# A graph network on one core: attention finishes each target tile inside its loop

## What is computed

```python
Q = (hn @ Wq).reshape(n, H, HD)          # K and V alike; hn = batch_norm(h)
score = jnp.clip(jnp.einsum('ehd,ehd->eh', K[src], Q[dst]) / np.sqrt(HD), -5.0, 5.0)
a = jnp.exp(score - smax[dst])
a = a / asum[dst]
wV = segment_sum(V[src] * a[:, :, None], dst, num_segments=n).reshape(n, DIM)
h2 = h_in1 + wV @ Wo + bo
h3 = _batch_norm(h2, bn2_g, bn2_b)       # statistics over all nodes
h3 = jax.nn.relu(h3 @ W1 + b1) @ W2 + b2
return h2 + h3                           # then a layer norm, and the last layer
```

## Time and profile before

| | |
|---|---|
| median of three runs (lowest to highest) | 1334.77 us (1333.79 to 1335.28) |
| profiled execution, its own time | 1335.18 us |
| its span, first to last instruction | 1333.2 us |
| busy: TensorE, VectorE, ScalarE, GpSimd | 990.6, 867.2, 523.6, 413.0 us |
| first and last gather of the loop start at | 655.7 and 1175.5 us |

### The profile page before, as it was taken

How to read it: one execution, slowest core, us unless ns; L and a number is a source line. 1 busy time by engine, 2 the same in 40 slices (tenths; PEclk the granted TensorE clock), 3 DMA queues, 4 the chain that set the end, 5 groups by cost and what they waited for, 6 DMA issues and landing times. The chain is left out here.

```text
span 1333.2 us, 18242 instructions
## 1 busy us (share of the span) xinstructions
PE 990.6 (74%) x6074; PEld 622.3 (47%) x6074; DVE 867.2 (65%) x2126; ACT 523.6 (39%) x1007; POOL 413.0 (31%) x516
## 2 busy tenths in 40 slices
PE   1289989999999998894655565656656565557997
PEld 1168845645556454454433343434434333345554
DVE  4879946734434467466377877777877777764343
ACT  1289913111111111112456555556655556424210
POOL 4000000000000000001277777777777777720000
PEclk9999999999999999896865766666666766568999
DMA  6000061000000000000543333333333333319000
GB/s 156 26 1 1 1 211 34 1 9 0 9 1 0 17 16 23 12 1 24 154 123 104 106 106 104 106 105 106 107 105 106 107 105 105 107 44 226 12 24 26
DMA packets 49496, 87.78 MB, mean 66 GB/s; under 512 B 12384, under 2 KB 35315, under 8 KB 49161
## 3 DMA queue, kind: packets, MB, share of 16 engines
q0 software_dynamic: 20608, 55.20, 14.4%
q1 hardware_dynamic: 26312, 29.89, 8.3%
q10 hardware_dynamic: 2492, 1.61, 0.5%
HBM read 70.68 MB, written 15.98 MB: 65 GB/s over the span
## 5 line engine op out<-in xcount | busy, mean ns | idle before, releaser
L1413 POOL DMA_INDIRECT counts_all<-kv_d,counts_all x416 | 394.4, 948 | 154.7 <-issue 145.9
L867 PE MATMUL bank<-counts_all,parts 125*128 (+2 forms) x1750 | 344.4, 355 | 19.5 <-DVE parts L1047 9.7
L867 PEld LDWEIGHTS bank<-counts_all,parts 125*128 125x128 f16 x1750 | 159.8, 98 | 190.9 <-DVE parts L1047 11.0
L1553 PE MATMUL bank<-counts_all 125*128 125x128 f16 x1230 | 133.9, 288 | 83.3 <-ACT counts_all L1619 82.9
L1299 POOL IOTA iota_n<- 128x256 f16 x1 | 0.3, 349 | 562.1 <-POOLq L854 562.1
L1553 PEld LDWEIGHTS bank<-counts_all 125*128 125x128 f16 x1230 | 110.1, 133 | 126.6 <-ACT counts_all L1619 126.3
L1542 PE MATMUL bank<-rel_rows,ident_h 104*128 104x512 f16 x104 | 56.9, 547 | 124.6 <-ACT away L1609 123.9
L1483 DVE TENSOR_TENSOR counts_all<-counts_all,bank 128x512 f32<-128x512 f32 x104 | 71.5, 687 | 117.6 <-DMA counts_all<-kv_d,counts_all 117.6
L1568 PE MATMUL bank<-counts_all,parts 128*128 128x272 f16 x615 | 135.2, 378 | 14.3 <-DVE counts_all L1461 12.1
L670 PE MATMUL bank<-parts 128*125 128x125 f16 x625 | 102.7, 324 | 12.0 <-DVE parts L589 12.0
L1609 ACT ACTIVATE away<-bank,lane_bias 125x512 f16<-125x512 f32 x173 | 110.8, 680 | 1.0 <-PE bank L1542 0.7
(11 more groups left out here) (268 smaller groups left out, 1264.2 us busy)
## 6 DMA issues: line engine op xcount, KB each, us to landing
counts_d<-counts_all SPq DMA_DIRECT2D x1, 6835.9 KB
counts_all<-counts_d SPq DMA_DIRECT2D x1, 6835.9 KB
counts_all<-kv_d,counts_all POOLq DMA_INDIRECT x416
kv_d<-counts_all SPq DMA_DIRECT2D x6, 448.0 KB
q_d<-counts_all SPq DMA_DIRECT2D x1, 1562.5 KB
x<-in_x SPq DMA_DIRECT2D x6, 250.0 KB
out<-parts SPq DMA_DIRECT2D x6, 250.0 KB
inv_deg<-in_x SPq DMA_DIRECT2D x1, 1400.0 KB
```

Of the source, the lines that this page charges most:

```text
L867: last = T.matmul(agg_ps[p][:, 0:w], pin[:, s, part, :], counts[:, s, bass.ds(b * BLK, w)], start=(s + part == 0), stop=(s + part == NT))
L1413: G.indirect_dma_start(out=out_rows, out_offset=None, in_=table_d, in_offset=bass.IndirectOffsetOnAxis(ap=index, axis=0)).then_inc(signal, 16)
L1553: last = T.matmul(pick_ps[n % DEEP][:, k * C:(k + 1) * C], ohT[n % DEEP][:, tile - GTILES[n][0], k, :], Q[:, tile, part, :], start=(tile = ...
```

## The change

Division, turning, projection and statistics move from the next stage into the loop. For a tile whose last group is L, ScalarE copies the high half in iteration L + 3 and VectorE adds the low half; VectorE divides in L + 4; TensorE turns the tile in L + 6 and ScalarE copies it; TensorE projects it in L + 7 and ScalarE copies that; VectorE takes its statistics in L + 8. Tiles 0 to 22 get through in the loop, 23 and 24 (`LATE`) right behind it. `turn_ps` and `project_ps` are in the bank that the spread writes, so in those two iterations the spread goes behind ScalarE's copy. `Q` and the projected tiles `h2T` share the end of the counts' room, so the counts come back in four pieces, three behind an `ff_done`. The general path gets the same steps, written out for 25 tiles.

```diff
+        ARENA_END = NT * N - NT * 2 * C - (NT * N) % 16
+        turned_area = counts_all[:, ARENA_END:ARENA_END + NT * 2 * C]
+        Q = turned_area[0:TILE, :].rearrange("p (t h c) -> p t h c", h=2, c=C)
+        h2T = turned_area.bitcast(fp32).rearrange("p (t c) -> p t c", c=C)[:, :, 0:TILE]
...
+            TURN_AT = {LAST_OF[t] + 6: t for t in range(NT) if LAST_OF[t] + 7 < NG}
+            PROJECT_AT = {LAST_OF[t] + 7: t for t in range(NT) if LAST_OF[t] + 7 < NG}
+            STATS_AT = {LAST_OF[t] + 8: t for t in range(NT) if LAST_OF[t] + 8 < NG}
...
+            LATE = [t for t in range(NT) if LAST_OF[t] + 7 >= NG]
...
+            turn_ps, project_ps = ps[0][:, 0:TILE], ps[0][:, LANES:LANES + TILE]
...
+                    sp.dma_start(w1[:, :], W1).then_inc(ff_in, 16)
+                    sp.dma_start(w2[:, :, :], W2.rearrange("(j f) c -> f j c", j=2)).then_inc(ff_in, 16)
                     sp.wait_ge(cols_in, 16 * 7)
...
+                    def divide(tile):
+                        rden_st.run(V.tensor_scalar(rden, acc[:, tile, C:VW], 1e-20, att_scale[0:TILE, V_SCALE:V_SCALE + 1],
+                                                    ALU.max, ALU.mult))
+                        rden_st.run(V.reciprocal(rden, rden))
+                        wv = acc[:, tile, 0:C].rearrange("p (h c) -> p h c", h=HEADS)
+                        V.tensor_tensor(wv, wv, rden.unsqueeze(2).to_broadcast([TILE, HEADS, HD]), ALU.mult).then_inc(wv_ready, 1)
+
+                    def statistics(tile):
+                        dve.wait_ge(h2_copied, tile + 1)
+                        V.bn_stats(bst2[:, tile, :], h2T[:, tile, :]).then_inc(h2_stats, 1)
+
                     def take_tiles(n):
                         for tile in range(NT):
                             if LAST_OF[tile] == n:
-                                dve.wait_ge(seg_done, n + 1)
-                                high, low = (tile_ps[tile % 2][0:TILE, part, :] for part in range(2))
-                                V.tensor_copy(acc[:, tile, :], high).then_inc(tile_taken, 1)
                                 dve.wait_ge(tile_taken, 2 * tile + 1)
-                                V.tensor_tensor(acc[:, tile, :], acc[:, tile, :], low, ALU.add).then_inc(tile_taken, 1)
+                                V.tensor_tensor(acc[:, tile, :], acc[:, tile, :], tile_ps[tile % 2][0:TILE, 1, :],
+                                                ALU.add).then_inc(tile_taken, 1)
+
+                    def divide_taken(n):
+                        for tile in range(NT):
+                            if LAST_OF[tile] == n:
+                                dve.wait_ge(tile_taken, 2 * tile + 2)
+                                divide(tile)
...
+                            if g >= 4:
+                                divide_taken(g - 4)
+                            if g in STATS_AT:
+                                statistics(STATS_AT[g])
...
+                        divide_taken(NG - 4)
                         for n in range(NG - 3, NG):
                             take_tiles(n)
+                            divide_taken(n)
+                        for tile in range(len(STATS_AT), NT):
+                            statistics(tile)
...
+                        for tile in range(NT):
+                            divide(tile)
+                        for tile in range(NT):
+                            statistics(tile)
...
+                    def turn(tile):
+                        pe.wait_ge(wv_ready, tile + 1)
+                        if tile:
+                            pe.wait_ge(h2_copied, tile)
+                        T.transpose(turn_ps, acc[:, tile, 0:C], ident[0:TILE, 0:TILE]).then_inc(wvt_done, 1)
+
+                    def project(tile):
+                        pe.wait_ge(wvt_copied, tile + 1)
+                        if tile == 0:
+                            pe.wait_ge(cols_in, 16 * 7)
+                        T.matmul(project_ps, wo[:, :], wvT, start=True, stop=False)
+                        for part in range(2):
+                            last = T.matmul(project_ps, x2[:, tile, part, :], ident_a[0:TILE, 4, :], start=False, stop=(part == 1))
+                        last.then_inc(h2_done, 1)
...
-                            if g + DEEP + 1 < NG:
-                                spread(g + DEEP + 1)
-                            if g >= 2:
+                            ahead = g + DEEP + 1
+                            if g in TURN_AT or g in PROJECT_AT:
+                                pe.wait_ge(away_ready, min(ahead, NG))
+                                if g in TURN_AT:
+                                    turn(TURN_AT[g])
+                                else:
+                                    project(PROJECT_AT[g])
                                 sums(g - 2)
+                                if ahead < NG:
+                                    if g in TURN_AT:
+                                        pe.wait_ge(wvt_copied, TURN_AT[g] + 1)
+                                    else:
+                                        pe.wait_ge(h2_copied, PROJECT_AT[g] + 1)
+                                    spread(ahead)
+                            else:
+                                if ahead < NG:
+                                    spread(ahead)
+                                if g >= 2:
+                                    sums(g - 2)
                             if g + DEEP < NG:
                                 pick(g + DEEP)
                         sums(NG - 2)
                         sums(NG - 1)
+                        for tile in LATE:
+                            turn(tile)
+                            project(tile)
...
+                        for tile in range(NT):
+                            turn(tile)
+                            project(tile)
...
+                    def copy_turned(tile):
+                        act.wait_ge(wvt_done, tile + 1)
+                        S.copy(wvT, turn_ps).then_inc(wvt_copied, 1)
+
+                    def copy_projected(tile):
+                        act.wait_ge(h2_done, tile + 1)
+                        if tile == 0:
+                            act.wait_ge(b2_added, 1)
+                            act.wait_ge(q_out_done, 16)
+                        S.activation(h2T[:, tile, :], project_ps, ACT.Identity, bias=bcol6[:, 7:8]).then_inc(h2_copied, 1)
+
+                    def take_high(n):
+                        for tile in range(NT):
+                            if LAST_OF[tile] == n:
+                                act.wait_ge(seg_done, n + 1)
+                                S.copy(acc[:, tile, :], tile_ps[tile % 2][0:TILE, 0, :]).then_inc(tile_taken, 1)
...
+                            if g >= 3:
+                                take_high(g - 3)
+                            if g in TURN_AT:
+                                copy_turned(TURN_AT[g])
+                            if g in PROJECT_AT:
+                                copy_projected(PROJECT_AT[g])
                             if g + DEEP < NG:
                                 turned_one_hots(g + DEEP)
                         high_part(NG - 1)
+                        for n in range(NG - 3, NG):
+                            take_high(n)
+                        for tile in LATE:
+                            copy_turned(tile)
+                            copy_projected(tile)
...
-                    sp.dma_start(w1[:, :], W1).then_inc(ff_in, 16)
-                    sp.dma_start(w2[:, :, :], W2.rearrange("(j f) c -> f j c", j=2)).then_inc(ff_in, 16)
                     sp.dma_start(bias, b3g.unsqueeze(0).to_broadcast([3, C])).then_inc(fin_in, 16)
 
-                    sp.wait_ge(h2_copied, NBLK + 1)
+                    def bring_back(first, past):
+                        for rows in SPRAY:
+                            sp.dma_start(counts_all[rows, first * N:past * N],
+                                         counts_d[rows, (first - SPILL) * N:(past - SPILL) * N]).then_inc(counts_back, 16)
+
                     sp.wait_ge(bias_step, BIAS_STEPS)
-                    for rows in SPRAY:
-                        sp.dma_start(counts_all[rows, SPILL * N:NT * N], counts_d[rows, :]).then_inc(counts_back, 16)
+                    bring_back(SPILL, NT - 3)
+                    for k in range(3):
+                        tile_end = (NT - 2 + k) * N
+                        held = -(-(tile_end - ARENA_END) // (2 * C))
+                        sp.wait_ge(ff_done, min(-(-held * TILE // BLK), NBLK + 1))
+                        sp.wait_ge(counts_back, 32 * (k + 1))
+                        bring_back(NT - 3 + k, NT - 2 + k)
                     sp.wait_ge(hid_done, NBLK + 1)
                     sp.dma_start(w3, wt_d[:, 9, :]).then_inc(fin_in, 16)
...
+                            if s >= NT - 3:
+                                pe.wait_ge(counts_back, 32 * (s - NT + 5))
...
-                    turn(0, 4, 0)
-                    for b, d0, w, t0, nt in every:
```

(20 more changed lines are left out.)

96 lines of the change are left out of this document (39 added, 57 removed).

## The result

The changed kernel takes 1322.91 us (1321.95 to 1324.78, four runs) against 1334.72 us, a ratio of 0.9917 with a 95% interval of 0.9903 to 0.9931: 11.8 us faster, where 11.2 were forecast. The profiled execution took 1322.6 us, its span is 1320.6 us against 1333.2.

The account below looks back on a forecast made before the run. GpSimd's gathers pace the loop; behind it nothing hides the chain. Terms -13.6 (chain), +2.2 (jump), +0.2 (held products) sum to -11.2 us: profiled 1324.0, median 1323.6 us; range 1319 to 1329, chance 0.42.

Parts of the forecast that it names:

- The chain behind the loop: From VectorE's last add to ScalarE's square root: only tiles 23 and 24 remain, square root at 1191.2 not 1204.80, gain 13.6 us.
- The jump: At the loop's end, engines skip the written-out general path: 2.2 us more, between the short and long jumps; bounds 0 and 2.5.
- the rival without a price for it: At the loop's end, the longer jump costs nothing: 1321.4 us, or 1319.6 with one hidden block at full clock; chance 0.36.
- The clock: First two hidden-product blocks stay at half clock; one more or less at full clock, 1.8 us, goes into the range.
- The held products' new order: In the tail, 64 + 4 x 2 held products replace 32 + 4 x 10: long products start 0.2 us later; bounds 0.2 and 1.74.
- w3: Weight load behind tile 24's counts on SP's queue: 6.5 us, covered by 32 held products of 6.95 us, so no wait.
- its rival: w3 and tile 24 come late: TensorE waits 3.05 us, plus perhaps 2 at half clock, 1328.6 us; chance 0.12.
- The loop: Attention loop: GpSimd's gathers pace it at 5.0 us an iteration; VectorE's added 17 us, ScalarE's and TensorE's work cost nothing.
- The gap of 1.13 us an iteration: VectorE's wait for the gathers, 117.6 us in 104 products; the worst iteration adds 1.0 us to it.
- free while it fits into such gaps: In the attention loop, work added to VectorE, ScalarE and TensorE costs nothing while it fits their waits.
- the rival of VectorE holding up GpSimd: In the loop, VectorE's SBUF-only work stops gathers: 15.5 us, with statistics 23; 1339.1 us, chance 0.06.
- the new waits of ScalarE and TensorE: In the loop, the spread stands behind ScalarE's copy, 2.1 us late; the delay fits, cost nothing.

Follow-up runs that it names:

- without the cover: GpSimd issues three gathers of four from the fourth group on, in the kernel before and the changed kernel: 1221.86 and 1221.16 us.
- ten tiles: Changed kernel with the general path's finish written out for only the first 10 of 25 tiles: 1322.81 us in one run.

## Why the prediction came out

**The chain behind the loop** held nearly term by term. From the last add to the end of the statistics it gave 1189.65 - 1185.3 = 4.35 us (measured 4.29), then 0.28 + 2.2 = 2.48 us of stage change and jump (2.50), then 1.28 us of table load (1.28). **The jump**, between bounds of 0 and 2.5, is 2.2 us: the rival without a price for it falls. The interpolation that chose 2.2 was lucky in its manner, since ten tiles cost nothing where a slope gave 1.0 us; that the price is TensorE's jump, as the prediction had it, is not shown. **The clock** gave 0.38 us, inside the 1.8 allowed, but less than the 2.9 us by which that stretch scatters, so it is not shown to come from the change. **The held products' new order** cost 0.22 us for a forecast 0.2. **w3** caused no wait; its rival was sound in mechanism (a late w3 costs the wait and some 2 us of clock, as it said) and missed by an estimated 0.9 to 1.4 us.

**The loop** came out right for a reason that was only half of it. The cover is real: the added work took 13 us out of VectorE's wait (17 were forecast), and without the cover it cost 12.1 us. The gap of 1.13 us an iteration was read a little large, since 11.0 of the 117.6 us lie in the first two iterations; it is about 1.05. But "free while it fits into such gaps" is not enough: 0.4 us of clamps an iteration fit and cost 29 us when they stood ahead of the subtraction. The step that failed is the one against the rival of VectorE holding up GpSimd: it read the gathers' median and minimum beside 104 subtractions and said that the trace does not agree with a lock. The maximum in the same row, 1394 ns, was a held gather; the subtraction mostly misses the gathers' starts by about 0.1 us. The Trainium skill (SBUF — State Buffer, SBUF: two separate sides) has this rule, of an exclusive lock for the whole instruction. The runs bear the lock out, but not its length: the hold ends 0.60 us into a subtraction of 0.715, and a subtraction that starts 0.04 us or more behind a gather's start, while the gather of 0.95 us still runs, lasts at most 0.73. That the changed kernel escaped it is due to where its additions stand: behind the product with the values, so that the subtraction keeps its place. Its own products of two SBUF operands last 0.29 us, and only one of the 25 has a gather start inside it, 0.28 us behind its start; that gather is not longer. How much such a product can hold up a gather that starts earlier is not shown there. The 1.0 us by which the loop grew (520.9 us from the first gather to the last, 519.9 before) matches nine starts inside the 0.60 us in place of five, 1.9 us of holding in place of 0.9. That leaves nothing for the new waits of ScalarE and TensorE, which the prediction also put at nothing.

## What to carry to other kernels

Work added to an engine that waits is free only if it moves nothing that the pacing engine is sensitive to: ask what each instruction behind it now coincides with, and put additions behind the sensitive one. Read the maximum of a row, not only its median, before a contention is ruled out. A path that is never taken can still cost when the jump over it is long, so write it as a loop.

## What the runs showed of the hardware

- A gather on GpSimd that starts 0.031 to 0.57 us behind the start of a VectorE subtraction with two SBUF operands (0.715 us) is held until 0.60 us behind it (526 cases, within 0.03 us). One that starts 0.030 us or less behind it is not, and lengthens the subtraction to 0.75 to 0.79 us (24 cases). Of the 161 gathers in the changed kernel that start within 0.60 us in VectorE's one-hots and products with one operand in PSUM, none is longer than 1.0 us.
- Jumping over the written-out finish of 25 tiles costs 2.2 us, over that of ten nothing.
- The 64 KB of w3, issued right behind a piece of 0.78 MB, took 4.58 us from issue to landing; the loads of 128 KB in the earlier trace rows took 2.1.
- ScalarE's table for the square root was loaded twice, 1.28 us each, when a square root stood at the end of the loop's stage and another in the next.
